# The four adjacency passes of a graph kernel as one loop on each engine, with the embedding steps behind them

## What is computed

```python
edge_index = jnp.stack([src, dst])
h = jnp.maximum(_layernorm(x, axis=-1), 0.0)
x = x + _L0_gnn_ref(h, edge_weight, ...)     # A = zeros.at[src, dst].add(w); deg = A.sum(1); dinv A dinv, 2 layers
h = jnp.maximum(_layernorm(x, axis=-1), 0.0)
x = x + _L1_gnn_ref(h, edge_index, node_vec1, ...)   # 4 blocks: conditional norm, attention over the edges, norm, MLP
h = jnp.maximum(_layernorm(x, axis=-1), 0.0)
x = x + _L2_gnn_ref(h, edge_index, W, b, diffusion_weights)   # adj from the edges, 3 diffusion steps
h = jnp.maximum(_layernorm(x, axis=-1), 0.0)
x = x + _L3_gnn_ref(h, edge_index, edge_type_2, ...)  # w = einsum('rb,bio->rio', att, basis), 2 relations, 2 layers
```

## Time and profile before

| | us |
|---|---|
| median of 3 runs | 1031.22 |
| lowest, highest | 1031.07, 1033.98 |
| profiled execution | 1031.43 |
| its span, first to last instruction | 1029.6 |
| start to the end of pass 0 | 71.2 |
| end of pass 0 to the end of pass 3 | 122.7 |
| end of pass 3 to layer 0 | 29.5 |
| layer 0 and 1 of L0 | 98.8 |
| L1, L2, L3 | 707.4 |

### The profile page before, as it was taken

How to read it: one execution, slowest core, us unless ns; L and a number is a source line. 1 busy time by engine, 2 the same in 40 slices (tenths; PEclk the granted TensorE clock), 3 DMA queues, 4 the chain that set the end, 5 groups by cost and what they waited for, 6 DMA issues and landing times.

```text
span 1029.6 us, 14714 instructions
## 1 busy us (share of the span) xinstructions
PE 888.0 (86%) x4334; PEld 679.1 (66%) x4334; DVE 551.1 (54%) x1238; ACT 426.7 (41%) x697; POOL 206.5 (20%) x143
## 2 busy tenths in 40 slices
PE   4866574769996999989999899999999796799998
PEld 3644252547673786967868678777878464678877
DVE  6976374755348446655565545664546847420110
ACT  4965454423423475235732377234762131221110
POOL 2001101003043012440124301423112323011100
PEclk9996886859998999999999999999999898599799
DMA  5744536343246344463443534553435662020100
GB/s 182 161 98 106 127 78 166 95 117 107 64 127 167 88 130 118 134 160 88 131 115 112 145 95 122 129 165 83 128 118 159 188 170 66 0 82 1 41 11 31
DMA packets 39884, 113.41 MB, mean 110 GB/s; under 512 B 7986, under 2 KB 8498, under 8 KB 32152
## 3 DMA queue, kind: packets, MB, share of 16 engines
q1 hardware_dynamic: 21064, 75.88, 30.7%
q10 hardware_dynamic: 18768, 36.83, 10.8%
HBM read 105.35 MB, written 7.34 MB: 109 GB/s over the span
## 4 chain that ended last, share of the span: by engine, by line
PE 73%; DVE 11%; issue 8%; ACT 3%; PEldq 3%; DVEq 1%; DMA 1%; SPq 0%; PEld 0%; POOL 0%; ACTq 0%
PE ring L1476 36%; PE ring L1691 21%; PE ring L1539 9%; PE ring L1494 4%; PE mix_ps L1505 2%; PEldq L1575 1%; PEldq L1543 1%; DVE yp L1269 1%; DVE stats L976 1%; ACT yp L813 1%; DVE xl L1286 1%; DMA att<-in_L_gnn_att 1%; ACT yp L844 1%; DVE yp L1274 1%; DVE y L985 1%
## 5 line engine op out<-in xcount | busy, mean ns | idle before, releaser
L596 POOL TENSOR_TENSOR wl<-wraw,wh 128x2048 fp32r<-128x2048 f32 x35 | 160.8, 4599 | 576.7 <-ACT wh L656 576.7
L1539 PE MATMUL ring<-ohs,ohd 128*128 128x512 f32 x368 | 96.4, 423 | 27.0 <-DVE ohd L1099 17.4
L1539 PEld LDWEIGHTS ring<-ohs,ohd 128*128 128x128 f32 x368 | 74.8, 207 | 54.2 <-DVE ohd L1099 23.0
L1099 DVE SCALAR_TENSOR_TENSOR ohd<-iota,dstT,vals 128x256 fp32r<-128x256 f32 x184 | 79.2, 477 | 42.4 <-PEq L1555 26.9
L1505 PE MATMUL mix_ps<-quad,att_shift 120*32 120x512 f32 x512 | 72.9, 652 | 26.2 <-issue 24.9
L697 ACT ACTIVATE ohs<-iota,minus_srcT 128x512 fp32r<-128x512 f32 x80 | 55.8, 715 | 53.8 <-PEq L1555 25.2
L656 ACT ACTIVATE wh<-wraw 128x2048 fp32r<-128x2048 f32 x35 | 66.7, 1905 | 4.5 <-DMA wraw<-in_L_gnn_root 4.4
L963 DVE TENSOR_TENSOR qk_l<-ring,qk_h 128x512 fp32r<-128x512 f32 x32 | 21.8, 690 | 76.2 <-ACT qk_h L682 76.2
L682 ACT ACTIVATE yT_h<-ring 128x512 fp32r<-128x512 f32 x32 | 19.1, 598 | 99.2 <-PE ring L1494 99.2
L600 POOL TENSOR_TENSOR rstd<-ve,half 128x1 f32<-128x1 f32 x52 | 29.6, 572 | 148.2 <-DVE ve L981 148.2
L1476 PE MATMUL ring<-yT_h,wl 128*128 128x512 f32 x128 | 50.4, 394 | 0.0
(11 more groups left out here) (316 smaller groups left out, 2226.3 us busy)
## 6 DMA issues: line engine op xcount, KB each, us to landing
quad<-in_L_gnn_basis SPq DMA_DIRECT2D x64, 960.0 KB, 7.8
wraw<-in_L_gnn_m_w ACTq DMA_DIRECT2D x8, 1024.0 KB, 5.1
mix_scratch<-mixed SPq DMA_DIRECT2D x128, 32.0 KB, 3.9
wraw<-in_L_gnn_wv ACTq DMA_DIRECT2D x4, 1024.0 KB, 5.1
wraw<-in_L_gnn_wq ACTq DMA_DIRECT2D x4, 1024.0 KB, 5.6
wraw<-in_L_gnn_wk ACTq DMA_DIRECT2D x4, 1024.0 KB, 5.3
wraw<-in_L_gnn_wo ACTq DMA_DIRECT2D x4, 1024.0 KB, 5.2
wraw<-mix_scratch ACTq DMA_DIRECT2D x4, 1024.0 KB, 5.7
```

The lines of the kernel that those rows point to most:

```text
L596: g.tensor_tensor(wl[s][:], wraw[s][:], wh[s][:].bitcast(F32), ALU.subtract).then_inc(weight_lo, 1)
L1099: return v.scalar_tensor_tensor(out, at.unsqueeze(1).broadcast_to([P, 4, HALF]), dstT[:, e], vals[:, e, :].rearrange("p a b -> p (a b)").u ...
L1539: last = te.matmul(edge_ps[m][2 * r + j], marks, ohs[:, u, :], start=False, stop=False)
```

## The change

All engines now run the passes as one hardware loop over m, TensorE with a loop over the groups too. Everything that depended on m in Python is now a register: the bits, the offset of `iota`, the PSUM banks, the semaphore counts. `edge_bank(m, k)` gives banks 0, 1, 2 for even m and 6, 5, 4 for odd m; bank 3 is shared by all. The words any and both are no longer formed on VectorE but in registers from two loads. The banks are emptied half 1 first.

- The 16 mix groups of the passes use four slots, the fourth in the memory of `mask`, each with a semaphore of its own (`pass_loaded`). The set is taken by ScalarE after the banks are emptied.
- `att_shift` is formed by GpSimd.
- VectorE: angles now stand behind the norm statistics, selectors behind normalise, `silu_argument` behind the degrees, `silu` behind `An_l`, `stack_conditioning` in front of the counts of layer 0, `split_cond(0, 0)` in layer 1, `split_cond(1, 1)` behind the last `block_input`.
- TensorE: z1 behind the degree matmuls, z2 in front of the counts; the wait for the selectors (`sel_step` 8) moves from ahead of layer 0 to right behind the loop.
- ScalarE: `hw(0)` right behind the loop, `hw(1)` behind `An_h`, `hw(2)` behind the U tiles of layer 0. GpSimd: `low_weight(0)` behind the inverse roots, the other two behind the power of the degrees.
- SyncE loads the second conditioning weights behind all early mix groups.

The diff, cut:

```diff
-        edge_ps = [[ring[:, (2 + 4 * m + j) % RING, :] for j in range(4)] for m in range(NT)]
+        def edge_bank(m, k):
+
+            return (m & 1) * (RING - 1 - 2 * k) + k
...
+            def load_pass_group(m, k):
+
+                if m:
+                    sp.wait_ge(quad_used, (m - 1) * GROUPS + k + 1)
+                base = m * SET_ROWS
+                src = l3["basis"][0][:, base:base + SET_ROWS, :].rearrange("b (i x) n -> b i x n", i=QUADS)
+                sp.dma_start(pass_quad(k), src[:, :, k * ROWS_IN_GROUP:(k + 1) * ROWS_IN_GROUP, :]).then_inc(pass_loaded[k], 16)
...
-                if g == 18:
-                    load_cond(0, 1, 1)
-                    sp.wait_ge(pass_act, 4 * NT)
-                    sp.wait_ge(pass_dve, 5 * NT)
+                if g == 20:
+                    sp.wait_ge(pass_dve, DVE_EVICTS * (SETS_HELD + NT))
                     for r in range(2):
                         sp.dma_start(ct_d[r], CT[r][:]).then_inc(ct_stored, 16)
+            load_cond(0, 1, 1)
...
+            pool.wait_ge(att_step, 2)
+            pool.wait_ge(att_loaded, 64)
+            for l in range(2):
+                for r in range(2):
+                    c = slice(0, WINDOW - STRIP // 2) if r == 0 else slice(WINDOW - STRIP // 2, WINDOW)
+                    last = g.tensor_scalar(att_shift[0:QUADS * BASES, l, c], iota[0:QUADS * BASES, c], place[0:QUADS * BASES, r:r + 1],
+                                           att[0:QUADS * BASES, l, r:r + 1], ALU.is_equal, ALU.mult)
+            last.then_inc(att_step, 1)
...
-            for w in range(3):
-                low_weight(w, slot(w))
+            pool.wait_ge(const_ready, 3)
             for t in range(NT):
                 inverse_root(t, t)
+            low_weight(0, slot(0))
             pool.wait_ge(deg_step, 1)
             g.tensor_tensor(dg[:, 2, :], dg[:, 1, :], half[:], ALU.pow).then_inc(deg_pool, 1)
+            for w in (1, 2):
+                low_weight(w, slot(w))
...
+                act.wait_ge(pass_ready, m + 1)
+                for r in (1, 0):
+                    c = slice(r * HALF, (r + 1) * HALF)
+                    a.activation(CT[1][c, bass.ds(m, 1), :], ring[0:HALF, bass.ds(edge_bank(m, 2 * r + 1), 1), :], ACT.Copy).then_inc(pass_act, 1)
+                    a.activation(Araw[c, bass.ds(m, 1), :], ring[HALF:P, bass.ds(edge_bank(m, 2 * r), 1), :], ACT.Copy).then_inc(pass_act, 1)
                 take_set(m)
-                act.wait_ge(pass_ready, m + 1)
-                for r in range(2):
-                    c = slice(r * HALF, (r + 1) * HALF)
-                    a.activation(Araw[c, m, :], edge_ps[m][2 * r][HALF:P, :], ACT.Copy).then_inc(pass_act, 1)
-                    a.activation(CT[1][c, m, :], edge_ps[m][2 * r + 1][0:HALF, :], ACT.Copy).then_inc(pass_act, 1)
-
-                if m == 0:
-                    act.wait_ge(emb_step, 4)
-                    a.activation(rnd[:], noise[:], ACT.Sin, scale=TURN).then_inc(emb_act, 1)
-                if m == 1:
-                    act.wait_ge(tile_taken, pre.base + pre.at["z1"] + 1)
-                    a.activation(sil[0][:], sil[1][:], ACT.Exp, scale=-1.0).then_inc(emb_act, 1)
-                if m < 3:
-                    hw(m)
-
-
+
+            hw(0)
+            act.wait_ge(emb_step, 4)
+            a.activation(rnd[:], noise[:], ACT.Sin, scale=TURN).then_inc(emb_act, 1)
             for t in range(NT):
                 act.wait_ge(ln_xn, t + 1)
                 a.activation(hb_h[0][:, t, :], xn0[:, t, :], ACT.Relu).then_inc(h0_hi, 1)
+            act.wait_ge(tile_taken, mid.base + mid.at["z1"] + 1)
+            a.activation(sil[0][:], sil[1][:], ACT.Exp, scale=-1.0).then_inc(emb_act, 1)
...
+            hw(1)
...
+                if l == 0:
+                    hw(2)
...
-            v.tensor_copy(turn_bits[:], bits_f[:]).then_inc(table_ready, 1)
-            dve.wait_ge(table_ready, 10)
-            v.tensor_tensor(any_bits[:], turn_bits[:, 0:HALVES:2], turn_bits[:, 1:HALVES:2], ALU.bitwise_or)
-            v.tensor_tensor(both_bits[:], turn_bits[:, 0:HALVES:2], turn_bits[:, 1:HALVES:2], ALU.bitwise_and).then_inc(flags_ready, 1)
-
-            dve.wait_ge(const_ready, 3)
+            v.tensor_copy(turn_bits[:], bits_f[:]).then_inc(flags_ready, 1)
+
+            dve.wait_ge(const_ready, 1)
...
-            between = [(selectors_and_angles,), (silu_argument,), (silu,), (stack_conditioning, lambda: split_cond(0, 0))]
-            for m in range(NT):
-                first_half = dve.value_load(turn_bits[0:1, 2 * m:2 * m + 1], min_val=0, max_val=2 ** TURNS - 1)
-                any_half = dve.value_load(any_bits[0:1, m:m + 1], min_val=0, max_val=2 ** TURNS - 1)
-                both_halves = dve.value_load(both_bits[0:1, m:m + 1], min_val=0, max_val=2 ** TURNS - 1)
+            with dve.Fori(0, NT) as m:
+                lower = dve.value_load(turn_bits[0:1, bass.ds(m * 2, 1)], min_val=0, max_val=2 ** TURNS - 1)
+                upper = dve.value_load(turn_bits[0:1, bass.ds(m * 2 + 1, 1)], min_val=0, max_val=2 ** TURNS - 1)
+                any_half, both_halves = dve.snap(lower | upper), dve.snap(lower & upper)
                 with dve.Fori(0, TURNS // SPAN) as g:
-                    some_turns(m, g, first_half, any_half, both_halves)
-                for step in between[m]:
-                    step()
+                    with dve.If(((any_half >> (g * SPAN)) & (2 ** SPAN - 1)) > 0):
+                        with dve.Fori(0, SPAN) as q:
+                            turn(m, g * SPAN + q, lower, any_half, both_halves)
+                    with dve.Else():
+                        dve.drain().then_inc(dst_ready, SPAN * BODY)
...
-                for r in range(2):
+                for n, r in enumerate((1, 0)):
                     c = slice(r * HALF, (r + 1) * HALF)
-                    v.tensor_copy(Csum[c, m, :], edge_ps[m][2 * r][0:HALF, :]).then_inc(pass_dve, 1)
-                    dve.wait_ge(pass_act, 4 * m + 2 * r + 1)
-                    v.tensor_tensor(Araw[c, m, :], edge_ps[m][2 * r + 1][HALF:P, :], Araw[c, m, :], ALU.add).then_inc(pass_dve, 1)
-                dve.wait_ge(pass_act, 4 * m + 4)
-                dve.wait_ge(pass_dve, 5 * m + 4)
-                v.tensor_tensor(CT[0][:, m, :], Csum[:, m, :], CT[1][:, m, :], ALU.subtract).then_inc(pass_dve, 1)
+                    v.tensor_copy(Csum[c, bass.ds(m, 1), :], ring[0:HALF, bass.ds(edge_bank(m, 2 * r), 1), :]).then_inc(pass_dve, 1)
+                    dve.wait_ge(pass_act, m * ACT_EVICTS + (SETS_HELD * ACT_EVICTS + 2 * n + 2))
+                    v.tensor_tensor(Araw[c, bass.ds(m, 1), :], ring[HALF:P, bass.ds(edge_bank(m, 2 * r + 1), 1), :],
+                                    Araw[c, bass.ds(m, 1), :], ALU.add).then_inc(pass_dve, 1)
+                dve.wait_ge(pass_dve, m * DVE_EVICTS + (SETS_HELD * DVE_EVICTS + 4))
+                v.tensor_tensor(CT[0][:, bass.ds(m, 1), :], Csum[:, bass.ds(m, 1), :], CT[1][:, bass.ds(m, 1), :], ALU.subtract
...
+            angles()
             for t in range(NT):
                 normalise(xn0[:, t, :], x[:, t, :], t, t)
+            selectors()
...
+            silu_argument()
...
-            split_cond(1, 1)
...
+            silu()
...
                 if l == 0:
+                    stack_conditioning()
+                    dve.wait_ge(emb_step, 9)
                     counts(0)
                     counts(1)
+                else:
+                    split_cond(0, 0)
...
             block_input(NT - 1)
+            split_cond(1, 1)
...
+            with pe.Fori(0, NT) as m:
+                lower = pe.value_load(turn_bits[0:1, bass.ds(m * 2, 1)], min_val=0, max_val=2 ** TURNS - 1)
+                upper = pe.value_load(turn_bits[0:1, bass.ds(m * 2 + 1, 1)], min_val=0, max_val=2 ** TURNS - 1)
+                any_half, both_halves = pe.snap(lower | upper), pe.snap(lower & upper)
+                banks = [pe.snap(edge_bank(m, k)) for k in range(3)] + [3]
+                pe.wait_ge(pass_act, m * ACT_EVICTS + ACT_EVICTS)
+                pe.wait_ge(pass_dve, m * DVE_EVICTS + DVE_EVICTS)
+                for k in range(3):
+                    te.matmul(ring[:, bass.ds(banks[k], 1), :], zero_l[:], zeros, start=True, stop=False)
+                pe.wait_ge(pass_act, m * ACT_EVICTS + (ACT_EVICTS + 2))
+                pe.wait_ge(pass_dve, m * DVE_EVICTS + (DVE_EVICTS + 2))
+                te.matmul(ring[:, 3, :], zero_l[:], zeros, start=True, stop=False)
+                with pe.Fori(0, TURNS // SPAN) as g:
                     with pe.If(((any_half >> (g * SPAN)) & (2 ** SPAN - 1)) > 0):
...
-                for ps in edge_ps[m]:
-                    last = te.matmul(ps, zero_l[:], zeros, start=False, stop=True)
+                    pe.wait_ge(att_step, 3)
+                    mix_in_pass(m, g)
+                for k in range(4):
+                    last = te.matmul(ring[:, bass.ds(banks[k], 1), :], zero_l[:], zeros, start=False, stop=True)
```

(14 more changed lines are left out.)

153 lines of the change are left out of this document (76 added, 77 removed).

## The result

The changed kernel takes 1042.92 us in the median of 4 runs (1041.53 to 1045.28), the kernel before 1031.14 (1029.66 to 1033.98): slower, ratio 1.0113, 95% interval 1.0084 to 1.0142. Forecast were 1027.5 us and a range up to 1037. The profiled execution took 1043.37 us, 11.9 more than that of before.

A forecast was written before the change was run, and what follows sets the result against it. VectorE's row was taken to set the time ahead of layer 0, TensorE's behind it, with stalls filling the gaps. 20.7 us saved less 16.8 given back made 3.9, so 1031.43 became 1027.5 us, range 1021 to 1037.

The forecast's parts named there:

- The gaps: Between passes: stalls at branches, read as code loads, vanish in the loop, saving 6.5, 6.6 and 5.4 us.
- the passes themselves: Inside the four passes, without the gaps: length carried over unchanged, no term in the sum, 0 us.
- The start: Ahead of pass 0: VectorE skips the attention coefficients' wait, att_shift and one word's load, 2.2 us earlier.
- Each quad still has a pass to land in: Basis rows in four slots cost nothing, up to 3 us if a shorter pass catches up with them.
- Behind the passes: Last pass to degree scaling: 33.8 us against 20.3 before, 13.5 us given back.
- the wait for the selectors: Behind the pass loop: TensorE's wait exposes a cold mix group, 1.93 us, and the degree matmuls, 6.96 us.
- the meeting with GpSimd's subtraction: Behind the passes: low_weight(0) holds up one VectorE operation, angles or normalise, priced at 4.3 us, bounds 0 and 4.3.
- The silu under layer 0: Moved behind An_l, into 5.60 us where VectorE sits idle ahead of layer 0's first low part: costs nothing.
- z2: On TensorE in front of the counts of layer 0, where its row is the bound: costs 1.1 us.
- The signs: Trace marks named beforehand, such as shorter gaps and layer 0 at about 216; one-half turns over 5 us would refute.
- the second rival: Code still has to be loaded, engines stall at back edges or code-skipping branches: 1033 to 1046 us, chance 0.17.
- The third: Rival: banks by register make each edge matmul dearer to issue; at 0.25 us more each, 1064 us, chance 0.04.

The follow-up runs named there:

- e7: The changed kernel, passes still a loop, with ScalarE's copy of the finished set ahead of the emptying of the banks: median 1043.07 us, ratio 1.0108.
- e6: As e4, passes written out, with ScalarE's copy of the finished set again ahead of the emptying of the banks: median 1046.85 us, ratio 1.0140.
- e4: The changed kernel with the passes and TensorE's groups written out on every engine, all moves kept: median 1033.73 us, ratio 1.0017.
- e8: The kernel before, with ScalarE's copy of the set behind the emptying of the banks in passes 0 and 2 alone: median 1025.71 us, ratio 0.9943.
- e3: The changed kernel with TensorE's four groups written out inside the loop over the passes, so mix groups need no If: median 1034.68 us, ratio 1.0027.
- e10: As e9, with SyncE ordering the first four groups of basis rows ahead of the first conditioning weights: median 1015.82 us, ratio 0.9844.
- e1: The changed kernel with TensorE's wait for the selectors back ahead of layer 0, behind the degree matmuls: median 1035.27 us, ratio 1.0026.
- e2: The changed kernel with GpSimd's three weight subtractions behind the last An_l: median 1035.91 us, ratio 1.0040.
- e9: The changed kernel with the edits of e1, e2 and e3, plus split_cond(1, 1) ahead of the H stage of layer 1: median 1016.59 us, ratio 0.9849.
- e11: As e10, with the passes written out again on every engine: median 1015.24 us, ratio 0.9835.

## Why the prediction was wrong

**The gaps: right in size, half right in cause.** Forecast 10.3, 14.1 and 13.2 us, measured 10.9, 13.8 and 13.0. I took the stalls for loads of code, and said that the loop ends them. It does: with the set copied ahead, the second and third gap are 13.8 and 13.0 us in the loop (e7) and 21.1 and 17.8 written out (e6). No row names a load; that the long branches are one rests on this and on the 33 packets of instructions against 21. What I missed is that a branch of 5 to 8 us was that long for the basis rows ordered just ahead of it, and that the change moved the copy of the set as well. That move is enough without the loop: e4 has all moves and no loop, and gaps of 10.2, 15.2 and 13.1; e8 makes it in two passes of the old kernel, and gains 5 us. In the first gap the long wait is VectorE's, and goes with the embedding steps in its passes (before and e8 against e4 and e6); no run parts the steps from the other moves there. My walk of VectorE (emptying, loads, skips) was the right model of a gap without stalls.

**The step that failed: the passes themselves.** I carried their length over as unchanged, and the sum has no term for it. It came to +13.0 us. From the shown rows: 10.0 in pass 0, made up of the wait for basis rows (1.6), longer pauses behind two mix groups (1.0 and 1.3), the turn, the mix group and the closing matmuls at the low clock (1.6, 0.9, 0.9), the pause between the last two mix groups (1.1), a middle at a granted clock of 0.92 (39.6 to 60.9, 0.9) and some 0.7 of smaller ones. The order of the changed kernel showed the branches between the mix groups. I priced them at nothing, since I had looked at VectorE alone as the engine that sets the pace; e3 takes 7.1 us of the 13 away by removing them, the walk and the low clock behind it together. The rest is not the walk: 5.1 us of it are there in e4 too. The wait for basis rows is one part (1.8 in e4). The low clock at the end of pass 0 is another, and it can come without the change, as the 3.0 us of e8's trace show. The rest is not split further.

**The start: right, and half given back.** 2.4 us earlier, but the first basis rows came no earlier than SyncE's queue let them. "Each quad still has a pass to land in" overlooked the very first. e10 removes the wait; what it is worth in time, these runs can't tell.

**Behind the passes: right.** 33.8 us forecast to the scaling, 33.7 measured (the terms as written give 28.9 and not 28.6 behind the degrees, so 0.3 us of the match is luck), with its two dear terms each shown by a run: the wait for the selectors 9.6 us (e1), the meeting with GpSimd's subtraction 4.2 (e2, forecast 4.3). The silu under layer 0 and split_cond(0, 0) show no cost, split_cond(1, 1) 1.9 (2.2). Layer 0 to the counts had z2 right at 1.05 us and 0.9 more at the low clock: its first 13 matmuls took 0.63 us or more each, 8 before. The pause right ahead of them is 4.15 us in both kernels; why the clock stays low for longer, no run tells.

**The signs.** The gaps, the one long VectorE operation, and the degrees behind the selectors came as foretold. Layer 0 began at 228.9 us and not at about 216, and one turn took over 5 us (5.50), which I had named as a sign against the forecast; it came from the clock behind a pause and not from the banks by register.

**The rivals.** The time fell in the span of the second rival, 1033 to 1046, but not through it: no branch of the loops took longer than 233 ns, as the 225 ns row said. The third finds no support: 64 matmuls with banks by register took 14.82 us in e9 and 14.79 by number in e4. **What stays open:** the 2.6 us behind the first block, of which 1.4 lie in one of four equal blocks; runs of the changed kernel themselves lie 3.8 us apart. Open too is why VectorE's long wait in the first gap goes with the embedding steps.

## What to carry to other kernels

When a change moves much and takes a loop in the bargain, undo the headline alone, and undo each companion alone too: here the loop or one moved line each shortened two of the gaps, so neither shows what it is worth while the other stands. Two other moved lines and the walk through the loop took the gain away. Before a difference between two traces is put down to an edit, compare their granted clocks in that stretch. A wait that an engine passes early in its stream exposes all that is queued behind it, so put it right ahead of its first user. A branch on the engine that multiplies has two costs: its own time, and the clock of what comes behind the pause.

## What the runs showed of the hardware

- Loads of code, as I read the long branches, and bulk transfers collide. The same branches took 2.5 and 3.5 us with the rows ordered behind them (e4) and 7.5 and 4.9 with the rows ahead (e6). Where no code is loaded, a DMA share of 0.89 changed a gap by nothing (e7). The Trainium skill, "Runtime: NRT & Kernel Launch", section "Instruction fetch mechanics", names the stall at a branch that leaves the window; the long branches agree. It says too that kernels prefer full unrolling where possible. The traces are divided on this: written-out groups in place of Ifs shortened the passes by 7.1 us (e3), while the loop over the passes loads 24 packets of instructions (e10) and written-out passes 33 (e11) in the same time.
- VectorE and GpSimd hold each other up in both directions: L1087 took 4.60 us instead of 0.42 beside a subtraction, and GpSimd's power on 4 columns 3.85 us instead of 1.0 beside hb_l. The Trainium skill, "SBUF — State Buffer", section "Who interferes with whom", gives this as a lock held for a whole instruction. The 4.60 us agree. The 3.85 are longer than any single VectorE operation beside it (0.6 to 0.7): the power ended 0.9 us behind the last of the four operations of hb_l, so it waited through the whole row of them.
- A pause of 2 us on TensorE ahead of 16 matmuls (63.95) went with 5.50 us for them at a granted clock of 0.69, one of 1.2 us (e3, 61.79) with 3.93 at 1.00. The pause right ahead does not settle it alone: behind 0.89 us the same 64 matmuls took 16.37 us in e3 and 14.82 in e9.
